# One LayerNorm buffer instead of two in the output projection of a transformer block, with the softmax reciprocals and the statistics' throwaway output moved

## The reference

```python
# attention: 16 heads of 64, windows of 512 tokens, each query sees a band of 512 keys back
q, k = rope(h @ Wq.T + bq), rope(h @ Wk.T + bk)
v = h @ Wv.T + bv
x = x + layernorm(banded_attention(q, k, v, 512) @ Wo.T + bo)
# channel mix: h_prev is h moved by one token
xr = mu_r * h + (1 - mu_r) * h_prev
xk = mu_k * h + (1 - mu_k) * h_prev
x = x + layernorm(sigmoid(xr @ W_r.T) * (square(relu(xk @ W_k.T)) @ W_v.T))
```

## Time and profile before

| | us |
|---|---|
| Median of the runs timed before | 5591.95 (2 runs, 5587.62 to 5596.29) |
| The profiled execution's own time | 5580.06 |
| Span of the profiled execution on its slowest core (core 6) | 5578.4 |
| Spans of the eight cores | 5551.1 to 5578.4 |

### The profile page before, as it was taken

How to read it: one execution, slowest core, us unless ns; L and a number is a source line. 1 busy time by engine, 2 the same in 40 slices (tenths; PEclk the granted TensorE clock), 3 DMA queues, 4 the chain that set the end, 5 groups by cost and what they waited for, 6 DMA issues and landing times.

```text
span 5578.4 us, 54149 instructions; the slowest of 8 cores (5551.1 to 5578.4 us)
## 1 busy us (share of the span) xinstructions
PE 3184.6 (57%) x11840; PEld 1238.2 (22%) x11840; DVE 2527.8 (45%) x3689; ACT 2120.3 (38%) x3905; POOL 1066.2 (19%) x900
## 2 busy tenths in 40 slices
PE   0345737558373774737746374773837367373773
PEld 0112213223121321313212131231312122131221
DVE  2354534445364453544536354443544544354452
ACT  0142533525333362433623344262433426343362
POOL 0021211212112121221211122121221212122121
PEclk9957568576685857658576775856658585675856
DMA  6613022130221303113021311303113130311301
GB/s 190 165 32 96 25 69 83 33 104 15 76 76 52 99 11 90 51 53 98 22 87 43 91 60 46 106 8 91 53 53 98 46 106 1 94 58 46 106 8 61
DMA packets 251425, 376.92 MB, mean 68 GB/s; under 512 B 149730, under 2 KB 149730, under 8 KB 251108
## 3 DMA queue, kind: packets, MB, share of 16 engines
q1 hardware_dynamic: 185060, 163.72, 11.7%
q0 software_dynamic: 33792, 134.22, 7.7%
q10 hardware_dynamic: 32256, 75.51, 3.5%
HBM read 264.33 MB, written 75.50 MB: 61 GB/s over the span
## 4 chain that ended last, share of the span: by engine, by line
PE 34%; DVE 21%; ACT 19%; issue 8%; DMA 7%; POOL 5%; SPq 3%; ACTq 2%; DVEq 1%; POOLq 0%
PE pb L479 8%; ACT pk L451 7%; PE pb L444 5%; DVE ybuf L491 5%; PE pb L393 4%; ACT vext L253 4%; ACT vext L250 4%; PE pb L633 4%; PE pb L658 3%; PE pb L535 3%; DVE ax L594 3%; SPq L171 3%; POOL pk L462 2%; POOL ybuf L708 2%; DVE qx L590 2%
## 5 line engine op out<-in xcount | busy, mean ns | idle before, releaser
L491 DVE RECIPROCAL ybuf<-pb 1x512 bf16<-1x512 f32 x256 | 858.0, 3352 | 744.0 <-PE pb L479 735.4
L451 ACT ACTIVATE pk<-pb,neg 128x512 bf16<-128x512 f32 (+3 forms) x1792 | 945.2, 527 | 282.9 <-PE pb L444 32.5
L633 PE MATMUL pb<-WS,qx 128*128 128x512 bf16 x1024 | 296.3, 455 | 1319.0 <-DVE qx L601 1100.4
L444 PE MATMUL pb<-qx,krot 64*128 64x512 bf16 (+3 forms) x1792 | 673.3, 431 | 311.2 <-ACT pk L451 255.9
L479 PE MATMUL pb<-pk,vext 128*65 128x128 bf16 (+3 forms) x2368 | 523.0, 404 | 78.7 <-DVE ax L504 38.8
L633 PEld LDWEIGHTS pb<-WS,qx 128*128 128x128 bf16 x1024 | 111.0, 113 | 1501.1 <-issue 1432.7
L466 POOL TENSOR_TENSOR pk<-pk,tri4s 128x512 bf16<-128x512 bf16 x256 | 294.7, 1151 | 749.1 <-ACT pk L451 749.1
L462 POOL TENSOR_TENSOR pk<-pk,tri0s 128x512 bf16<-128x512 bf16 x192 | 221.3, 1152 | 1106.9 <-ACT pk L451 1106.9
L342 PE MATMUL pb<-hfm,Wwq 128*128 128x512 bf16 x1024 | 253.6, 405 | 306.7 <-DMA hfm<-hstage 228.2
L479 PEld LDWEIGHTS pb<-pk,vext 128*65 128x65 bf16 x2368 | 309.1, 170 | 255.4 <-issue 171.5
L444 PEld LDWEIGHTS pb<-qx,krot 64*128 64x128 bf16 x1792 | 165.6, 107 | 872.9 <-issue 872.3
(11 more groups left out here) (97 smaller groups left out, 3837.1 us busy)
## 6 DMA issues: line engine op xcount, KB each, us to landing
xsl<-x SPq DMA_DIRECT2D x128, 512.0 KB, 3.8
WS<-wo_bf POOLq DMA_DIRECT2D x16, 2048.0 KB, 11.3
WS<-wr_bf POOLq DMA_DIRECT2D x16, 2048.0 KB, 18.4
WS<-wk_bf POOLq DMA_DIRECT2D x16, 2048.0 KB, 11.3
WS<-wv_bf POOLq DMA_DIRECT2D x16, 2048.0 KB, 11.2
out<-ybuf ACTq DMA_DIRECT2D x64, 512.0 KB, 2.6
hstage<-htm ACTq DMA_DIRECT2D x64, 256.0 KB, 2.5
cosb<-cosd SPq DMA_DIRECT2D x64, 256.0 KB, 6.2
```

Source lines behind the costliest of these rows:

```text
L444: qlo=qlo, qhi=qhi: e.matmul(pb[bk][:, qlo:qhi], ksrc[po:po + 64, BS * md + 128 * tc:BS * md + 128 * (tc + 1)], qx[po:po + 64, BS * md + q ...
L451: texp = cop("scalar", lambda e, bk=bk, c=c, qlo=qlo, qhi=qhi, pku=pku: e.activation(out=pku[:, BS * c + qlo:BS * c + qhi], in_=pb[bk][:, ...
L491: t_rc = cop("vector", lambda e, rb=recipb[uslot], ub=ub: e.reciprocal(rb, pb[ub][64:65, :]), waits=[t_av, buf.get(("recip", uslot)), prev ...
L633: ins = e.matmul(pb[bk][:, :], qx[:, BS * ci + 128 * tj:BS * ci + 128 * (tj + 1)], WS[1][:, D * ci + BS * hh:D * ci + BS * (hh + 1)], star ...
```

## The change

Four edits.

1. `aof` is a single buffer. The copy of tile j (L544) now waits for the normalisation (L551) of tile j-1, and the wait is the same token in the feed-forward stage.
2. `recipb` moves from `ybuf` to the first row of `htm`. The first reciprocal of a block waits for the write of `htm` to `hstage`, where it waited for the last output store, and the first new write of `htm` names the last matmul that reads the reciprocals.
3. `lnsink` becomes 1024 bfloat16 elements, where it was 1024 float32.
4. The six statistics tiles exist once, and no token guards them.

```diff
-    aof = [sb("aof0", [128, D], F32), pk2[1][:, 2048:4096].bitcast(F32)]
+    aof0 = sb("aof0", [128, D], F32)
+    aof = [aof0, aof0]
-    recipb = [ybuf[0:1, 256 * i:256 * (i + 1)].bitcast(BF16) for i in range(2)]
+    recipb = [htm[0:1, BS * i:BS * (i + 1)] for i in range(2)]
...
-    lnt = [dict(ssum=sb("ssum%d" % i, [128, 1], F32), nmt=sb("nmt%d" % i, [128, 1], F32),
...
+    ssum = sb("ssum", [128, 1], F32)
...
-            waits=list(waits) + [buf.get(("lnset", si))], tok=True)
+            waits=list(waits), tok=True)
...
-        lnsink[0] = vext[1 - par][:, 0:2048].bitcast(F32)
+        lnsink[0] = vext[1 - par][:, 0:1024]
...
-                rb, pb[ub][64:65, :]), waits=[t_av, buf.get(("recip", uslot)), prev_z], tok=True)
+                rb, pb[ub][64:65, :]), waits=[t_av, buf.get(("recip", uslot)), t_hw[-1]],
+                tok=True)
...
                 tev = cop("scalar", lambda e, sl=sl, hh=hh, bk=bk: e.copy(
                     aof[sl][:, BS * hh:BS * (hh + 1)], pb[bk][:, :]),
-                    waits=[tmm, buf.get(("aof", sl))], tok=True)
+                    waits=[tmm, buf.get("aof")], tok=True)
...
-            buf[("aof", sl)] = tt1
-            buf[("lnset", tj)] = tt1
+            buf["aof"] = tt1
...
                 tfe = cop("vector", lambda e, sl=sl, hh=hh, pin=pin, rap=rap: e.tensor_mul(
                     aof[sl][:, BS * hh:BS * (hh + 1)], pin, rap),
-                    waits=[tmm, buf.get(("aof", sl))] + t_rsg, tok=True)
+                    waits=[tmm, buf.get("aof")] + t_rsg, tok=True)
```

More of the change, by code:

```diff
@@ L150, in build_core @@
     h2last = sb("h2last", [128, 8], BF16)
-    lnt = [dict(ssum=sb("ssum%d" % i, [128, 1], F32), nmt=sb("nmt%d" % i, [128, 1], F32),
-                svt=sb("svt%d" % i, [128, 1], F32), vart=sb("vart%d" % i, [128, 1], F32),
-                sdt=sb("sdt%d" % i, [128, 1], F32), rst=sb("rst%d" % i, [128, 1], F32))
-           for i in range(4)]
+    ssum = sb("ssum", [128, 1], F32)
+    nmt = sb("nmt", [128, 1], F32)
+    svt = sb("svt", [128, 1], F32)
+    vart = sb("vart", [128, 1], F32)
+    sdt = sb("sdt", [128, 1], F32)
+    rst = sb("rst", [128, 1], F32)
     pb = [st.enter_context(nc.psum_tensor("pb%d" % i, [128, BS], F32)) for i in range(8)]
@@ L243, in build_core, with ln_stats @@
     lnsink = [None]
-    def ln_stats(xap, waits, si):
+    def ln_stats(xap, waits):
         sink = lnsink[0]
-        T = lnt[si]
-        ssum, nmt, svt = T["ssum"], T["nmt"], T["svt"]
-        vart, sdt, rst = T["vart"], T["sdt"], T["rst"]
         t1 = cop("scalar", lambda e, sink=sink: e.activation(
             out=sink, in_=xap, func=AF.Identity, accum_out=ssum[:, :]),
-            waits=list(waits) + [buf.get(("lnset", si))], tok=True)
+            waits=list(waits), tok=True)
         t2 = cop("scalar", lambda e, sink=sink: e.activation(
@@ L263, in ln_stats @@
         t6 = cop("vector", lambda e: e.reciprocal(rst[:, :], sdt[:, :]), waits=[t5], tok=True)
-        return t6, nmt, rst
+        return t6
     def stream_weight(wn, slot, after):
@@ L295, in planA @@
                           xin[rows0a + 128 * j: rows0a + 128 * (j + 1), :], waits=w)
-            t_rs, nmt, rst = ln_stats(xsl[sl][:, :], [t_x1[j]], j)
-            t_ln[j] = cop("vector", lambda e, sl=sl, j=j, nmt=nmt, rst=rst: e.tensor_scalar(
+            t_rs = ln_stats(xsl[sl][:, :], [t_x1[j]])
+            t_ln[j] = cop("vector", lambda e, sl=sl, j=j: e.tensor_scalar(
                 htm[:, D * j:D * (j + 1)], xsl[sl][:, :], nmt[:, :], rst[:, :], ALU.add, ALU.mult),
                 waits=[t_rs, buf.get("htm")], tok=True)
-            buf[("lnset", j)] = t_ln[j]
         t_hw = [dma("scalar", "hw", hstage[128 * j:128 * (j + 1), :], htm[:, D * j:D * (j + 1)],
@@ L503, in plan_norm @@
             buf[("recip", uslot)] = t_bc
+            buf["recip_all"] = t_bc
             t_ae = cop("vector", lambda e, md=md, po=po, bb=bb, u=usb[uslot]: e.tensor_mul(
@@ L549, in build_core @@
             sl = tj % 2
-            t_rs, nmt, rst = ln_stats(aof[sl][:, :], t_oev, tj)
-            tt1 = cop("vector", lambda e, sl=sl, nmt=nmt, rst=rst: e.tensor_scalar(
+            t_rs = ln_stats(aof[sl][:, :], t_oev)
+            tt1 = cop("vector", lambda e, sl=sl: e.tensor_scalar(
                 scr[:, :], aof[sl][:, :], nmt[:, :], rst[:, :], ALU.add, ALU.mult),
                 waits=[t_rs, buf.get("scr")], tok=True)
-            buf[("aof", sl)] = tt1
-            buf[("lnset", tj)] = tt1
+            buf["aof"] = tt1
             t_y[tj] = cop("gpsimd", lambda e, sl=sl, tj=tj: e.tensor_add(
@@ L566, in build_core @@
         for j in range(4):
-            t_rs, nmt, rst = ln_stats(ybuf[:, D * j:D * (j + 1)], [t_y[j]], j)
-            th2j = cop("vector", lambda e, j=j, nmt=nmt, rst=rst: e.tensor_scalar(
+            t_rs = ln_stats(ybuf[:, D * j:D * (j + 1)], [t_y[j]])
+            t_h2.append(cop("vector", lambda e, j=j: e.tensor_scalar(
                 htm[:, D * j:D * (j + 1)], ybuf[:, D * j:D * (j + 1)], nmt[:, :], rst[:, :],
-                ALU.add, ALU.mult), waits=[t_rs, t_hw[-1]], tok=True)
-            t_h2.append(th2j)
-            buf[("lnset", j)] = th2j
+                ALU.add, ALU.mult),
+                waits=[t_rs, t_hw[-1], buf.get("recip_all") if j == 0 else None], tok=True))
         t_h2w = [dma("scalar", "hw", h2stage[128 * j:128 * (j + 1), :], htm[:, D * j:D * (j + 1)],
@@ L701, in build_core @@
             sl = tj % 2
-            t_rs, nmt, rst = ln_stats(aof[sl][:, :], t_fev, tj)
-            tt1 = cop("vector", lambda e, sl=sl, nmt=nmt, rst=rst: e.tensor_scalar(
+            t_rs = ln_stats(aof[sl][:, :], t_fev)
+            tt1 = cop("vector", lambda e, sl=sl: e.tensor_scalar(
                 scr[:, :], aof[sl][:, :], nmt[:, :], rst[:, :], ALU.add, ALU.mult),
                 waits=[t_rs, buf.get("scr")], tok=True)
-            buf[("aof", sl)] = tt1
-            buf[("lnset", tj)] = tt1
+            buf["aof"] = tt1
             tz = cop("gpsimd", lambda e, sl=sl, tj=tj: e.tensor_add(
```

## The result

The changed kernel is slower by 1.1%: ratio 1.0112 of the kernel before, 95% interval 1.0068 to 1.0155 (medians 5650.87 us of 11 runs and 5597.43 us of 10). At 5597 us that ratio is 63 us, with an interval of 38 to 87; forecast were 54 us on the median then known, 5646 us.

A forecast was written before the change was run, and what follows sets the result against it. No engine exceeds 57% busy, so a chain of handoffs bounds the kernel, with ACT and DVE pacing the Wo stage. 57.0 less 3 x 0.96 gives +54 us on the 5591.95 median: 5646 us, range 5622 to 5684.

The forecast's parts named there:

- The single buffer in the Wo stage: Wo stage: first copies of tiles 1 to 3 delayed by the new wait, 3.56 us a block, 57.0 us total.
- The 0.96 us taken back in slow blocks: Wo stage, tile 2: in 3 blocks with slow matmuls, slack absorbs 0.96 us each, bringing 57.0 to 54.1 us.
- Nothing behind takes it back: After the Wo stage, from LayerNorm through transposes and mix to L633, no slack recovers the delay: 0 us recovered.
- The three small edits at nothing: Reciprocals in htm, single statistics set, bfloat16 throwaway output: 0 us taken; the output's ends were -18 to +28 us.
- Rival A: Wo stage, tiles 2 and 3: TensorE at half clock becomes the bound; 66 us more, 5712 us; chance 0.07.
- the slack computed for it: Wo stage: second copy can start at 7.0 us, TensorE ready at 5.1 at full clock; covers about 1.6 us slowness.
- Rival B: Hole before the h2stage transposes swallows the delay, 3.4 us a block; time stays at 5592 us; chance 0.07.

The follow-up runs named there:

- wait_for_add: Kernel before, both aof buffers kept; copies of tiles 1 to 3 also wait for POOL's addition of the tile before; ratio 1.0273 to before.
- rest_only: Changed kernel with the second aof buffer given back in both stages, the three small edits kept; ratio 1.0024 to the kernel before.
- four_banks_after: Changed kernel with the Wo stage's matmuls on PSUM banks 0 to 3 in turn instead of 0 and 1; ratio 1.0131 to the kernel before.
- pipelined: Kernel before with same-semaphore wait tokens merged, four PSUM banks in Wo stage, next tile's copies or passes ahead of the square root; 0.9645 of before, 5389 us.

## Why the prediction was right

- **The single buffer in the Wo stage** was the main cost, by the mechanism forecast. The steps of 1.14, 1.21 and 1.21 us, added up because each normalisation depends on its own copies, made 3.56 us a block. Measured over all cores they are 1.15, 1.20 and 1.19, together 3.54. (a) grew by 3.46: less the 0.21 of the next point, and with 0.13 in small pieces, of which tile 0's wait for TensorE is 0.07.
- **The 0.96 us taken back in slow blocks** was right, with some luck in its size. The forecast counted three such blocks on one core, 0.18 us a block; the cores of before had between 1 and 8, 3.4 on average, and the second copy of tile 2 indeed comes 0.21 us earlier. With it the sum was 54.1 us; the ruler gives 55.4 us over all cores and 53.5 on die 0.
- **Nothing behind takes it back.** (b), (c) and (d) are each within 0.15 us of before, and wait_for_add showed the same at three times the dose.
- **The three small edits at nothing** were right but for about 5 us: rest_only gave 1.0024 with 1 in its interval, and passes of 1057 ns in place of an unseen shape that could have been 1022 or 1112, but the stretch from the mix to the first sigmoid is 0.3 us a block longer wherever these edits are. The forecast had no term for it, and its cause is open.
- **Rival A** had its first half right. TensorE's idle time before tile 2 went to 3.3 us or more, and the clock in tile 2 was down not in 3 but in 13 of 16 blocks on the slowest core (on all cores 14.9 on average, against 3.4 before). TensorE's wait before tile 3, which the rival put at 1.9 us, was 1.93 in the three blocks with a fast tile 2 and mostly 0.33 in the others, because slow matmuls of tile 2 filled it. On the slowest core it stopped short of costing anything, as the slack computed for it (7.0 less 5.1 us) said, and four_banks_after confirmed it. Only on cores 6 and 7, whose clock was 0.687, did the second copy of tile 2 wait for matmuls in six blocks each, mostly by 0.25 us and once by 1.2. The rival's full price was added up a little low: 2.1 us times 32 is 67, not 66.
- **Rival B** fell by its own counter-argument, 0.05 us for each old wait: the trace has the waits at 0.050 us each, the changed kernel has the same hole, and taking the waits out closed it.
- The point estimate was 54 us and the comparison gives 63 with an interval from 38 to 87. The 9 us between them are less than the measurement can tell. The spans of die 0 are 63 us apart too: 53.5 lie in (a), 5 between the mix and the first sigmoid, and the rest is spread over the other stages in small pieces.

## What to carry to other kernels

In a queue that works in order, a second buffer is worth what lies between the last reader's end and the moment at which the writer's own queue would have let it start, here 1.2 us of a 5.08 us step. Read it off as the end of the reader plus the handoff, less the start of the writer, and ask whether the queue order lets the buffer do more; here moving the copies ahead of the square root, with four PSUM banks, drew a further 1.9 us a block from the same buffer. The line of the Trainium skill that the prediction cites ("Trainium Kernel Development and Optimization", "Best Practices") speaks of overlapping DMA with compute. Here one engine fills the buffer and others read it, and ACT's order had already barred most of the overlap. Where a hole in the chain shows no instruction and its length goes with the number of tokens in a wait list, merge the tokens: that was worth 2.1%, twice what the buffer was.

## What the runs showed of the hardware

- **A wait that was already met cost 0.050 us on SP.** 143 of them filled 7.49 us and 79 filled 4.31, and merging them left 0.21 us with 4.
- **DVE's subtraction of two SBUF tiles was held until POOL's addition had ended.** In the trace of before, 16 of the 256 subtractions on core 0 took longer than 0.2 us; each ended 0.02 us after a POOL addition, and none that overlapped one was short. In pipelined it was 64 of 256, up to 1.01 us for a 128x1 tile. Written as a TENSOR_SCALAR, the same subtraction took 0.21 us every time, beside the additions too. The Trainium skill, "SBUF — State Buffer", section "Who interferes with whom", says that a vector instruction with two SBUF inputs contends with a GpSimd instruction that reads SBUF. The traces agree, for a 128x1 subtraction against a 128x1024 addition of two SBUF tiles.
- **A lower TensorE clock can be free.** In tile 2 of the changed kernel it was down in 13 of 16 blocks on the slowest core, after idle times of 3.3 to 3.6 us, and no copy of that tile came later for it. After 2.15 us of idleness, in the kernel before, it was down in 1 to 8 blocks of 16, depending on the core.
